# A new order for the prologue of a gated cross-attention and mixture-of-experts kernel

## The reference

```python
x = x + tanh(g_xattn[0]) * xattn(_layernorm(x), ctx_1024, W_kv, W_q, W_proj, b_proj)
x = x + tanh(g_ffn[0]) * ffn(_layernorm(x), gate_w, w_up, w_down, sg_gate, sg_up, sg_down)
# xattn: 16 heads of 16, K and V from the context, Q from x
attn = softmax(einsum('bhqd,bhkd->bhqk', q, k) * SCALE)
out = einsum('bhqk,bhkd->bhqd', attn, v).reshape(B, Nq, C) @ W_proj + b_proj
# ffn: the two best of 8 experts per token, silu(g) * u @ w_down, and a shared expert
```

## Time and profile before

| | us |
|---|---|
| median of the runs | 592.05 |
| the profiled execution | 597.62 |
| its span | 594.4 |
| busy in the span: TensorE, DVE, ACT, GpSimd | 531.9, 304.4, 233.4, 140.5 |
| first product of the maxima of unit 0 | 66.07 |
| first exponential (slot 0) | 92.91 |
| first exponential of slot 1 | 107.68 |

### The profile page before, as it was taken

How to read it: one execution, slowest core, us unless ns; L and a number is a source line. 1 busy time by engine, 2 the same in 40 slices (tenths; PEclk the granted TensorE clock), 3 DMA queues, 4 the chain that set the end, 5 groups by cost and what they waited for, 6 DMA issues and landing times.

```text
span 594.4 us, 8011 instructions
## 1 busy us (share of the span) xinstructions
PE 531.9 (89%) x2393; PEld 285.8 (48%) x2393; DVE 304.4 (51%) x611; ACT 233.4 (39%) x430; POOL 140.5 (24%) x169
## 2 busy tenths in 40 slices
PE   0899777999999999996989999899999999999980
PEld 0455312333333333332449656456777777777750
DVE  4375793788778787873447441223333333333320
ACT  2344314777777777773653211011221221222210
POOL 7073000000110000100000046711333333333332
PEclk9999856999999999998998599999999999999995
DMA  8237990565565267374000013322333433333322
GB/s 282 80 97 252 243 363 38 152 177 154 165 183 151 78 206 206 104 232 118 11 2 0 2 57 128 136 89 73 61 63 53 64 63 54 56 65 59 54 27 26
DMA packets 52654, 65.73 MB, mean 111 GB/s; under 512 B 6800, under 2 KB 44432, under 8 KB 52112
## 3 DMA queue, kind: packets, MB, share of 16 engines
q1 hardware_dynamic: 33440, 39.84, 23.7%
q0 software_dynamic: 7152, 9.34, 9.6%
q10 hardware_dynamic: 12032, 16.17, 8.5%
HBM read 37.93 MB, written 27.20 MB: 110 GB/s over the span
## 4 chain that ended last, share of the span: by engine, by line
PE 65%; DMA 12%; DVE 8%; SPq 5%; issue 4%; ACT 2%; ACTq 1%; POOLq 0%; DVEq 0%; POOL 0%
PE ps L852 51%; PE ps L920 9%; DMA out<-unit_region 8%; DVE neg_max L658 3%; DMA unit_region<-nm_parts 2%; SPq L296 2%; SPq L286 2%; DVE slot_rows L607 2%; PE ps L1141 1%; DMA gates<-in_g_ffn 1%; PE ps L1121 1%; ACT ctx_region L513 1%; PE ps L928 1%; DVE unit_region L834 1%; PE ps L1031 1%
## 5 line engine op out<-in xcount | busy, mean ns | idle before, releaser
L658 DVE TENSOR_REDUCE neg_max<-ps 128x2 f32<-128x1024 f32 x128 | 150.9, 1219 | 43.2 <-PE ps L852 43.2
L513 ACT ACTIVATE ctx_region<-ps 128x512 f32<-128x512 f32 x256 | 141.4, 596 | 76.8 <-PE ps L852 75.6
L852 PE MATMUL ps<-unit_region 96*128 96x512 bf16 (+1 forms) x512 | 147.0, 401 | 18.8 <-DMA unit_region<-nm_parts 8.6
L852 PEld LDWEIGHTS ps<-unit_region 96*128 96x128 bf16 (+1 forms) x512 | 46.2, 99 | 134.2 <-ACT ctx_region L513 67.8
L852 PE MATMUL ps<-up_region,unit_region 128*128 x312 | 107.1, 486 | 0.0
L437 POOL DMA_INDIRECT out<-unit_region x39 | 60.6, 1553 | 138.1 <-DMA out<-unit_region 77.8
L852 PE MATMUL ps<-dn_region,unit_region 128*128 (+1 forms) x330 | 78.4, 380 | 3.3 <-issue 2.7
L852 PEld LDWEIGHTS ps<-dn_region,unit_region 128*128 128x128 f32 x330 | 62.5, 190 | 21.7 <-issue 5.3
L852 PEld LDWEIGHTS ps<-up_region,unit_region 128*128 128x128 f32 x312 | 56.2, 190 | 31.0
L920 PE MATMUL ps<-ctx_region,unit_region 128*32 128x512 f32 x512 | 69.9, 619 | 0.7 <-ACT ctx_region L513 0.7
L826 DVE TENSOR_TENSOR unit_region<-unit_region,ps 128x384 f32<-128x384 f32 x39 | 21.6, 554 | 77.2 <-ACT unit_region L572 74.3
(11 more groups left out here) (118 smaller groups left out, 454.0 us busy)
## 6 DMA issues: line engine op xcount, KB each, us to landing
up_region<-in_w_upT ACTq DMA_DIRECT2D x9, 768.0 KB, 4.3
qk_parts<-up_region SPq DMA_DIRECT2D x32, 192.0 KB, 5.3
unit_region<-qk_parts SPq DMA_DIRECT2D x32, 192.0 KB, 4.3
x_slots<-empty ACTq DMA_DIRECT2D x1, 5031.0 KB, 18.4
unit_region<-x_slots SPq DMA_DIRECT2D x39, 129.0 KB
v_rows<-dn_region SPq DMA_DIRECT2D x4, 1024.0 KB, 6.6
unit_region<-qk_parts SPq DMA_DIRECT2D x32, 128.0 KB, 4.3
unit_region<-v_rows SPq DMA_DIRECT2D x16, 256.0 KB, 4.6
```

Of the source, the lines that this page charges most:

```text
L513: nc.scalar.activation(probs[:, k % 8, :], bank(4 + k % 2), ACT.Exp).then_inc(exp_done, 1)
L658: nc.vector.tensor_reduce(neg_max[:, s, 2 * p:2 * p + 2], bank(2 * (p % 2), 2), AX.X, ALU.max, negate=True).then_inc(max_done, 1)
L852: return nc.tensor.matmul(o_, w, m, start=start, stop=stop)
```

## The change

K and V of a batch are projected before the turn and Q, in halves, and batch 0 and 1 run through so; from batch 2 on a pair of score tiles of units 0 and 1 (`first_pair`) stands between two halves. 36 transposes of the identity (`WARM`) open TensorE's list. From batch 1 on DVE computes only a shift (`ln_shift`), and ACT applies it (`apply_rows`). The low parts of batches 2 and 3 are on GpSimd. SP loads K, then Q, of units 0 and 1 as soon as batch 0 has been sent, then V of these two, and then the other two units; the first maxima follow the sends of batch 2. V has a semaphore of its own (`v_in`), the sends of a batch have two (`kv_out`, `q_out`). The x of batch 0, the weights of Q and the small inputs are loaded through ACT's queue, K's and V's weights in separate transfers. tanh and the scaling of the bias move to the end of the prologue, the additions of the bias between the splits of the maxima. Two small buffers move into `unit_region`.

```diff
-QK_ORDER = [(a, b) for b in range(B) for a in (0, 1)]
-OUTS = 2 * (H // 4) + 1
+QK_ORDER = [(a, b) for b in range(B) for a in (1, 0)]
+KV_OUTS, Q_OUTS = H // 4 + 1, H // 4
-LOADS = len(K_RUNS) + len(Q_RUNS) + 1
+LOADS = len(K_RUNS) + len(Q_RUNS)
+        K_BANK, V_BANK = 4, 6
+        XT_BANK, Q_BANK = (0, 0, 4, 4), (2, 2, 6, 6)
...
@@ SP
+            sp.dma_start(wkv_sb[:, :, 0:D], w_kv_rows[:, :, 0:D]).then_inc(wk_in, 16)
+            load_ctx(0)
+            sp.dma_start(wkv_sb[:, :, D:2 * D], w_kv_rows[:, :, D:2 * D]).then_inc(wv_in, 16)
+            for b in range(1, B):
+                load_ctx(b)
+                sp.dma_start(x_sb[:, b * TB:(b + 1) * TB, :], x_dram[:, b * TB:(b + 1) * TB, :]).then_inc(x_in[b], 16)
...
-            send_max(0, 0)
+            send_k(0)
+            send_v(0)
+            sp.wait_ge(kv_out[0], 16 * KV_OUTS)
+            for g in range(2):
+                load_rows(0, g, 1, k_unit, K_RUNS)
+            send_q(0)
+            sp.wait_ge(q_out[0], 16 * Q_OUTS)
+            for g in range(2):
+                load_rows(0, g, 0, q_unit, Q_RUNS)
+            for g in range(2):
+                load_v(0, g)
+            for g in range(2, NG):
+                load_rows(0, g, 1, k_unit, K_RUNS)
+                load_rows(0, g, 0, q_unit, Q_RUNS)
+                load_v(0, g)
             for b in range(1, B):
-                sp.wait_ge(qkv_out[b], 16 * OUTS)
+                send_k(b)
+                send_v(b)
+                send_q(b)
+                if b == 2:
+                    send_max(0, 0)
+            for b in range(1, B):
+                sp.wait_ge(kv_out[b], 16 * KV_OUTS)
+                sp.wait_ge(q_out[b], 16 * Q_OUTS)
...
@@ GpSimd
             pool.wait_ge(const_step, 9)
+            pool.wait_ge(rows_done, 1)
             nc.gpsimd.memset(v_sb[:, :, :, :, HD:VW], 1.0).then_inc(v_ones, 1)
...
+            low_part(1, 2)
+            low_part(0, 2)
+            split_max(0)
+            low_part(1, 3)
+            low_part(0, 3)
+            pool.wait_ge(bias_done, 1)
             for u in range(UNITS):
-                split_max(u)
+                if u >= 1:
+                    split_max(u)
+                if u < NT // 2:
+                    add_bias(2 * u)
+                    add_bias(2 * u + 1)
...
@@ ACT
+            def apply_rows(b):
+                act.wait_ge(shift_done, b)
+                for t in range(b * TB, (b + 1) * TB):
+                    last = nc.scalar.activation(rows[:, t, :], x_sb[:, t, :], ACT.Identity, bias=shift[:, t:t + 1],
+                                                scale=rstd[:, t:t + 1])
...
+            for b in range(B):
+                high_k(b)
+                if b == B - 1:
+                    copy_first_max()
+                copy_xnT(b)
+                mid_part(1, b)
+                copy_v(b)
+                if b + 1 < B:
+                    std_of(b + 1, b + 2)
+                    apply_rows(b + 1)
+                high_q(b)
+                mid_part(0, b)
+            act.wait_ge(gates_in, 16 * 2)
+            nc.scalar.activation(tanh_g[:, :], gates[:, :], ACT.Tanh).then_inc(tanh_done, 1)
...
@@ DVE (ln_stats(0), ln_apply(0), resid_part(1, 0), ln_stats(1), low_part(1, 0), ln_shift(1), ln_stats(2) ahead)
+            resid_part(0, 0)
+            low_part(0, 0)
+            resid_part(1, 1)
+            ln_shift(2)
+            low_part(1, 1)
+            dve.wait_ge(x_in[3], 16)
+            ln_stats(3, 4)
+            resid_part(0, 1)
+            low_part(0, 1)
...
+            max_pair(0, 0, 0)
+            max_pair(0, 1, 0)
+            resid_part(1, 2)
+            ln_shift(3)
+            max_pair(0, 2, 0)
...
+            max_pair(0, 5, 0)
+            resid_part(0, 2)
+            max_pair(0, 6, 0)
+            max_pair(0, 7, 0)
+            resid_part(1, 3)
+            for p in range(5):
+                max_pair(1, p, 1)
+            resid_part(0, 3)
...
@@ TensorE
+            for i in range(WARM):
+                nc.tensor.transpose(bank(7)[:, 0:P], ident[:, :], ident[:, :])
...
+            for b in range(2):
+                project_k(b, 0)
+                project_k(b, 1)
+                project_v(b, 0)
+                turn_xn(b)
+                project_v(b, 1)
+                project_q(b, 0)
+                project_q(b, 1)
...
+            project_k(2, 0)
+            first_pair(0, 0)
+            project_k(2, 1)
+            first_pair(0, 1)
+            project_v(2, 0)
+            first_pair(0, 2)
+            turn_xn(2)
+            first_pair(0, 3)
+            project_v(2, 1)
+            first_pair(0, 4)
+            project_q(2, 0)
+            first_pair(0, 5)
+            project_q(2, 1)
+            first_pair(0, 6)
+            project_k(3, 0)
+            first_pair(0, 7)
+            project_k(3, 1)
+            turn_max(0, 0)
+            project_v(3, 0)
+            first_pair(1, 0)
+            turn_xn(3)
+            first_pair(1, 1)
+            project_v(3, 1)
+            first_pair(1, 2)
+            project_q(3, 0)
+            first_pair(1, 3)
+            first_pair(1, 4)
+            project_q(3, 1)
+            first_pair(1, 5)
+            first_pair(1, 6)
+            first_pair(1, 7)
```

More of the change, by code:

```diff
@@ L143, in build @@
         rstd = sb("rstd", [P, NT])
+        shift = sb("shift", [P, NT])
         neg_max = sb("neg_max", [P, 2, P])
@@ L219, in build @@
         low_done = sem("low_done")
-        qkv_out = [sem(f"qkv_out{b}") for b in range(B)]
+        kv_out = [sem(f"kv_out{b}") for b in range(B)]
+        q_out = [sem(f"q_out{b}") for b in range(B)]
         unit_in = [sem(f"unit_in{s}") for s in range(4)]
+        v_in = [sem(f"v_in{s}") for s in range(4)]
         pair_ps = sem("pair_ps")
@@ L269, in _, with load_ctx @@
         def _(sp):
[L270 to L274 removed]
+            def load_ctx(b):
                 sp.dma_start(ctx_sb[:, :, b * T:(b + 1) * T],
@@ new lines, in load_rows, with load_v @@
+            def load_rows(b, g, a, dst, runs):
+                row = 0
+                for run in runs:
+                    n = len(run)
+                    src = qk_parts[a, bass.ds(b, 1), g, 0:n, :, :].rearrange("a j (d h) n -> (a j d) (h n)", h=HG)
+                    to = dst[row:row + n * HD, g, :, :].rearrange("p h n -> p (h n)")
+                    sp.dma_start(to, src).then_inc(unit_in[g], 16)
+                    row += n * HD
+            def load_v(b, g):
+                src = v_rows[bass.ds(b, 1), :, :, g * HG * VW:(g + 1) * HG * VW].rearrange("a p k c -> p (a k) c")
+                sp.dma_start(v_unit[:, g, :, :], src).then_inc(v_in[g], 16)
@@ L296, in _, with send_k, send_v, send_q @@
                     sp.dma_start(qk_parts[a, b, g, :, :, :].rearrange("j r n -> r j n"),
[L297 to L305 removed]
+                                 parts[half:half + P // 2, b, a, :, g // 2, :]).then_inc(done, 16)
+            def send_k(b):
+                send_parts(1, b, kv_out[b])
+            def send_v(b):
+                sp.wait_ge(v_done, b + 1)
+                sp.dma_start(v_rows[b, :, :, :], v_sb[:, b % 2, :, :, :].rearrange("p k h w -> p k (h w)")
+                             ).then_inc(kv_out[b], 16)
+            def send_q(b):
+                send_parts(0, b, q_out[b])
             def send_max(u, g):
@@ L670, in normalise @@
                                         ).then_inc(attn_rows, 1)
-            dve.wait_ge(const_step, 3)
-            for w in range(2):
-                for p in range(8):
-                    max_pair(w, p, w)
             for p in range(8):
@@ L876, in project_v, with project_q @@
-            def project_v(b):
-                if b >= 1:
-                    pe.wait_ge(v_done, b)
-                for kt in range(TB):
+            def project_q(b, c):
+                if c == 0:
+                    if b == 0:
+                        pe.wait_ge(wq_in, 16)
+                    pe.wait_ge(rowsT_sb, b + 1)
+                    if b == 1:
+                        pe.wait_ge(resid_done, QK_ORDER.index((0, 0)) + 1)
+                    elif b >= 2:
+                        pe.wait_ge(v_done, b + 1)
+                for d in range(DC):
+                    last = mm(bank(Q_BANK[b] + c), wq_sb[:, d, c * P:(c + 1) * P], xnT[:, d, b * T:(b + 1) * T],
+                              d == 0, d == DC - 1)
+                if c == DC - 1:
+                    last.then_inc(q_ps, 1)
@@ new lines, in project_k @@
+            def project_k(b, c):
+                if c == 0:
+                    if b == 0:
+                        pe.wait_ge(wk_in, 16)
+                    pe.wait_ge(ctx_in[b], 16)
+                    if b in (1, 2):
+                        pe.wait_ge(resid_done, QK_ORDER.index((1, b - 1)) + 1)
+                    elif b == 3:
+                        pe.wait_ge(rowsT_sb, 3)
+                for d in range(DC):
+                    last = mm(bank(K_BANK + c), wkv_sb[:, d, c * P:(c + 1) * P], ctx_sb[:, d, b * T:(b + 1) * T],
```

(16 more changed lines are left out.)

227 lines of the change are left out of this document (101 added, 126 removed).

## The result

The changed kernel takes 578.02 us (median of four runs, 577.37 to 580.26), the kernel before beside it 592.27: a ratio of 0.9765, interval 0.9737 to 0.9793. It is 14.2 us faster; forecast were 9.5 and a range of 578.5 to 588, so the time is just past the end of the range, where rival A stood (578.2). The profiled execution took 578.13, its span 576.4.

What follows compares the result with a forecast made beforehand. Projections, 19 us of maxima and SP's list were taken to stand in series before slot 0. First exponential at 83.4 in place of 92.91, 9.5 us earlier, gave 592.05 - 9.5 = 582.5 us; range 578.5 to 588.

Steps and rivals of the forecast that it cites:

- rival A: More is won: slot 0 at the upper clock level, 2.3 us shorter, and no 2.0 us for hand-overs: 578.2 us; chance 0.16.
- the round trip: Batch 0's K and Q sent to HBM and loaded back before the first pair of unit 0, ending at 42.3 us.
- the hand-overs: Some 20 hand-overs on the path to the first exponential, 0.05 to 0.3 us each: 2.0 us added.
- Part 3: Pairs of maxima between projections from 42.3 us to the first score at 80.4; 3.7 of clock, 5.9 of stops.
- The terms: Prices per instruction taken from profile rows; not shown there: normalising on ACT 1.6 us, low part on GpSimd 2.9 us.
- Part 1: Batches 0 and 1: warm-up transposes free TensorE at 9.8 us, Q of batch 1 ends at 32.3.
- Part 2: TensorE stops 8.3 us, 34.0 to 42.3, for unit 0's loads; up to 47 with late landings; clock falls, losing 3.7.
- Part 4: Slot 0 and after: slot 0 stays 14.8 us, slot 1's maxima are hidden, 9.5 us come off the median.
- B: The clock falls again in TensorE's 2.9 us stop at 53.9 us, costing 3.8: 586.3 us; chance 0.20 together with C.
- C: GpSimd's low parts at 6.8 us and slow sends and maxima delay slot 1: 589.0 us; chance 0.20 together with B.
- D: Slower: the low clock never leaves the stage of pairs between projections, first exponential at 101 us: 600 us; chance 0.08.
- E: Little changes, because K and Q of batch 0 come back 12 us beyond 42.3 and all slips; chance 0.04.

Runs made afterwards that it cites:

- d1: Changed kernel with the four low parts of batches 2 and 3 moved from GpSimd back to DVE: first exponential at 76.86 us, ratio to the kernel before 0.973.
- d4: Changed kernel with 36 identity transposes added in TensorE's stop for unit 0's loads: first exponential at 76.03 us, ratio to the kernel before 0.981.
- a1: Changed kernel without the 36 transposes that open TensorE's list: first exponential at 80.89 us, ratio to the kernel before 0.983.
- b1: Changed kernel with K's loads of units 0 and 1 waiting only for K's sends, V sent behind them: first exponential at 77.58 us, ratio to the kernel before 0.989.
- a4: Changed kernel with DVE reducing pairs 2 and 3 of unit 0 before batch 3's shift: first exponential at 73.08 us, ratio to the kernel before 0.967.
- a3: Changed kernel with K 2, V 2 and the turn of x 2 ahead of the first pair, later pieces moved up: first exponential 66.91 us, ratio to the kernel before 0.956.

## Why the prediction was off

The mechanism was right in each part; three terms of the sum for the first exponential were not, all too large: the start (2.2 us), the round trip (3.1) and the hand-overs (2.0). Part 3 gave 0.7 back. Together that is 6.6 us, the 83.4 forecast less the 76.78 measured. The steps that failed are these three, the start and the landing times first.

**The terms.** GpSimd's low part took 2.12 us (taken 2.9, 2.9 to 6.8 the bounds): below the lower bound. Four times a short instruction counts its start four times, if the two forms run at one rate. ACT's normalising took 2.08 (taken 1.6, upper bound 2.2). Neither size moved the sum: d1 shows it for the one, and for the other the rows were ready ahead of their turns. What no term had is the 0.46 us by which GpSimd's work stretched DVE's shift (d1).

**Part 1** was mis-sized by 2.2 us. It held K until 9.8 for the transposes; these took 6.09 us (8.2 were assumed), and K began at 7.65. The pace rose within them: 6 or 7 records touch each microsecond from 2.6 to 5.6, and 11 and 10 the next two. So by my estimate the upper level came some 4 us in, where the sum had 7.5. The price was also a little high: 36 at the upper level take 4.09 us (d4), and 4.9 were assumed. The step that failed is "the rise after some 7.5 us of work as at 92.3", one case taken for a rule. Shorter transposes would not have helped: a1 has the load of context 0 at 7.75. (The products of part 1 add up to 34.3 and not 34.0, which moves nothing, as the loads end the stop.)

**Part 2** was mis-sized by another 3.1 us. K's low part was done at 17.2 in place of 19.8 (2.2 of it inherited, 0.4 from a DVE low part of 1.23 and not 1.73, though the memset did run beside it); V's landing took 5.5 us, nearly as said (5.7); six loads of K were issued in 2.67 us, where I had put the middle of 2.8 and 4.6; Q's sends and their landing took 5.2, as said (5.1); and unit 0's loads landed 3.5 us after the first issue, not 5.3. Together 5.3 us: 37.01 for 42.3. The steps that failed are the six loads of K (1.0 us too much) and the landing of unit 0's loads (1.8). Both were taken from a stretch of the kernel before in which the DMA engines were busy throughout (DMA share 1.01 in 56 to 58); here it was 0.24 in 25 to 27 and 0.31 in 33 to 35. That the empty queue made them quicker fits b1, but no run varied it alone.

**Part 3** held within 0.8 us: forecast were 38.1 us from the first pair to the first score, with stops of 2.9 and 2.7; measured are 38.9, with 3.31 and 2.67. The fall of the clock cost 3.1 us in place of 3.7 (43.1 in place of 49.8, at 37.0 in place of 42.3). The waits named there are those of the trace: DVE behind ACT's square root (a4: 2.5 us of its 3.7), Q behind the copy of V, DVE's last residual.

**The 2.0 us for hand-overs** were an error of method: the durations were starts to ends from the trace, which hold most of the hand-overs already. From the first pair to the first exponential the trace has 39.8 us, and the sum without the term had 39.1. With the right start and without this term the sum gives 76.1, and the trace has 76.78.

**Part 4** held: slot 0 took 15.0 us (14.8 taken), nearly half of it at the low level, slot 1's maxima were hidden, one table load. In the Trainium skill, ScalarE: Activation LUTs, "Table sets: the hidden batching unit", exp and tanh are in one set; the one load at 75.37, and the exponential that starts 0.1 us after tanh (76.78 and 76.67), agree. Of the 16.1 us 13.5 were left at the end of the attention (297.14 in place of 310.61; the difference is within the spread of that stage), and 14.2 in the runs. So the time was 4.5 us off where the first exponential was 6.6 off.

**Rivals.** A's time came by luck, another way: slot 0 was not shorter, the prologue was. B didn't come here, but it came in five of the seven profiles with the same stop, so its chance was put too low, and that it stayed away was luck. In those five the fall cost 1.6 to 1.9 us of the first exponential; B had 3.8. C fell: GpSimd off the path, maxima at 64.26 and early enough. D fell: at half pace TensorE worked without a pause and the clock rose at 43. The gap after 67.1, which the prediction sets beside a wait for DMA, was a wait of 3.58 us for DVE. E fell. The range should have reached to 576: the ends of part 2 had been taken to the late side alone (47, never 37).

**Where the 16.1 us come from**, by what undoing costs: V's own semaphore 2.2 to 3.0, the opening transposes 2.2, the maxima's place in SP's list 8 to 9, the pairs between the projections 6.2 (with the maxima sent last), GpSimd's low parts 0. They overlap and don't add up. Against that stand two stops of 8.3 us together, which with the clock's fall a3 shows to be worth 9.9. The split between K-first, the early loads and ACT's normalising wasn't tried.

## What to carry to other kernels

When a chain is rebuilt by hand from a trace, its waits come out well and its start and its transfers badly: take both ends of each landing time, the early one too, and add nothing for hand-overs that the rows already hold. Where an in-order engine will stand for a round trip, look for work behind the wait that doesn't need it and put it ahead: here that won 9.9 us, on top of the 16.1 of the whole change. When one execution stands for a kernel, look first whether the clock fell in the same places: a gain or a loss of 1 to 2 us can be the clock's.

## What the chip showed that was not expected

One and the same stop of TensorE, 3.31 us long, left the granted clock at 2.4 GHz in two profiles and took it to 1.2 in five, for 1.1 to 1.5 us of loss in the product behind it; d4 kept the clock up through the stop before and then paid in this one. A DVE instruction on 128x4 elements took 0.63 us beside GpSimd's low part and 0.16 without it, in all eight profiles in which the two meet. A GpSimd tensor operation of 128x1024 took 2.12 us and one of 128x256 0.72; an estimate from the two, if both forms run at one rate, is a start of some 0.25 us. And removing SP's wait for V's send won nothing, since Q's sends then went out slowly behind V's megabyte (4.66 us in place of 2.62).
